# Weight copies moved behind the last attention pair, and both halves of a scatter moved ahead of it

## The reference

```
x = x + tanh(g_xattn) * attention(layernorm(x), ctx)      # 8 batches, 256 tokens, 128 wide, 16 heads of 64
logits = layernorm(x) @ Wr + br ;  i = argmax(logits)     # 8 experts, 512 hidden
out = sum over e of relu((xn * (i == e)) @ W1[e] + b1[e]) @ W2[e] + b2[e]
x = x + tanh(g_ffn) * out
```

## Time and profile before

| | us |
|---|---|
| median of 3 runs | 365.06 (364.78 to 365.91) |
| profiled execution | 365.85 |
| its span, first to last instruction | 363.8 |
| PE busy | 345.6 (95%) |
| DVE busy | 270.9 (74%) |
| ACT busy | 255.5 (70%) |
| POOL busy | 191.0 (52%) |
| mean granted TensorE clock | 0.998 |

### The profile page before, as it was taken

The page is one execution under the profiler, slowest core; times in us unless marked ns, Lnnn a source line. Parts: engine busy times, 40 slices in busy tenths (PEclk is TensorE's granted clock), DMA queues, the critical chain, the costliest instruction groups (busy, mean ns, idle before and its releaser), DMA issues.

```text
span 363.8 us, 11160 instructions
## 1 busy us (share of the span) xinstructions
PE 345.6 (95%) x2835; PEld 283.3 (78%) x2835; DVE 270.9 (74%) x1262; ACT 255.5 (70%) x936; POOL 191.0 (52%) x369
## 2 busy tenths in 40 slices
PE   8999999999999999999999999999999897978893
PEld 6776778778878787878778877887887666968893
DVE  4789995878687868786878687867777696776671
ACT  3686775887687868785878587859773667646562
POOL 7245555366537744774467436833681570345544
PEclk9999999999999999999999999999999999999999
DMA  6999202000400030004000400040005914133320
GB/s 201 248 367 244 91 2 90 4 2 1 122 0 0 0 119 0 0 0 119 0 0 0 119 0 0 17 117 0 0 29 211 366 36 133 50 104 105 89 66 13
DMA packets 21562, 27.87 MB, mean 77 GB/s; under 512 B 3649, under 2 KB 16789, under 8 KB 21536
## 3 DMA queue, kind: packets, MB, share of 16 engines
q1 hardware_dynamic: 19776, 23.85, 21.7%
q0 software_dynamic: 1504, 3.16, 2.5%
q10 hardware_dynamic: 256, 0.56, 0.5%
HBM read 19.00 MB, written 9.01 MB: 77 GB/s over the span
## 4 chain that ended last, share of the span: by engine, by line
PE 80%; DVE 10%; issue 3%; ACT 3%; DVEq 1%; DMA 1%; another core or an unknown queue 1%; POOLq 0%; SPq 0%; POOL 0%; ACTq 0%
PE ps_kv L1255 15%; PE ps_o L1255 13%; PE ps_s L1255 13%; PE ps_t L1359 11%; PE ps_w L1255 10%; PE ps_q L1255 8%; PE ps_t L1255 7%; DVE masked L823 2%; DVE prob_T L842 2%; PE ps_s L1479 1%; ACT prob L565 1%; PE ps_w L1396 1%; DMA nat<-in_ctx 1%; DVE row_fix L830 1%
## 5 line engine op out<-in xcount | busy, mean ns | idle before, releaser
L433 POOL TENSOR_SCALAR prob<-prob,row_inv 128x128 f32<-128x128 f32 (+1 forms) x256 | 104.8, 429 | 124.9 <-DVE row_inv L836 124.7
L565 ACT ACTIVATE prob<-masked,neg_max 128x128 f32<-128x128 f32 (+1 forms) x256 | 113.7, 447 | 65.5 <-DVE neg_max L823 65.2
L823 DVE CUSTOM_DVE_ANT_0 masked<-ps_s,mask_now 128x128 f32<-128x128 f32 (+1 forms) x256 | 77.8, 353 | 44.3 <-PE ps_s L1255 40.8
L842 DVE COPY prob_T<-ps_t 128x384 f32<-128x384 f32 x123 | 65.0, 549 | 0.8 <-PE ps_t L1359 0.7
L1255 PE MATMUL ps_s<-k_T,q_T 64*128 64x128 f32 (+1 forms) x512 | 59.6, 351 | 1.5 <-DVE neg_max L823 1.5
L1359 PEld LDWEIGHTS ps_t<-ident,prob 128*128 128x128 f32 x384 | 41.0, 141 | 21.5 <-issue 17.3
L1359 PE MATMUL ps_t<-ident,prob 128*128 128x128 f32 x384 | 56.1, 282 | 0.6 <-DVE prob_T L842 0.5
L1255 PE MATMUL ps_o<-prob_T,v_nat 128*64 128x256 f32 (+1 forms) x512 | 49.8, 333 | 2.1 <-DVE prob_T L842 1.5
L565 ACT ACTIVATION_READ_ACCUMULATOR prob<-masked,neg_max 128x1 f32 x256 | 48.5, 190 | 0.0
L1255 PEld LDWEIGHTS ps_o<-prob_T,v_nat 128*64 128x64 f32 x512 | 31.7, 136 | 16.3 <-issue 2.1
L1255 PEld LDWEIGHTS ps_s<-k_T,q_T 64*128 64x128 f32 x512 | 33.9, 188 | 9.7 <-issue 6.8
(11 more groups left out here) (200 smaller groups left out, 545.9 us busy)
## 6 DMA issues: line engine op xcount, KB each, us to landing
ctx_buf<-in_ctx SPq DMA_DIRECT2D x8, 768.0 KB
sorted_rows<-pad_rows SPq DMA_DIRECT2D x8, 642.5 KB, 4.4
tile_in<-sorted_rows SPq DMA_DIRECT2D x24, 128.5 KB, 2.1
packs<-in_L_ffn_W SPq DMA_DIRECT2D x1, 2048.0 KB
packs<-in_L_ffn_W SPq DMA_DIRECT2D x8, 256.0 KB
nat<-in_ctx SPq DMA_DIRECT2D x8, 128.0 KB, 3.4
nat<-in_x SPq DMA_DIRECT2D x1, 768.0 KB, 6.6
w_in<-in_L_xattn_Wk SPq DMA_DIRECT2D x2, 256.0 KB, 4.5
```

The source lines that it names most:

```text
L433: g.tensor_scalar(prob[:, slot, lo:hi], prob[:, slot, lo:hi], row_inv[:, slot, t:t + 1], 1.0, ALU.mult, ALU.mult).then_inc(prob_ready, 1)
L565: s.activation(prob[:, slot, lo:hi], masked[:, slot % 2, lo:hi], ACT.Exp, bias=neg_max[:, slot, t:t + 1], scale=-1.0, accum_out=row_sum[:, ...
L823: v.tensor_tensor_reduce(out=masked[:, slot % 2, lo:hi], in0=ps_s[slot % 2][:, lo:hi], in1=mask_now[:, lo:hi], scale=-SCALE, scalar=FLOOR, ...
L842: v.tensor_copy(prob_T[:, slot % TSLOTS, :], ps_t[slot % 2][:, 0:W3]).then_inc(probT_kept, 1)
```

## The change

Three moves; no work is added or taken away.

DVE: the w2 copies of tiles 0 to 3 come behind the copy of pair 63's first head. The other three leave the batch: tile 4's stands behind the second norm of batch 7, tile 5's behind `choose`, tile 6's behind `place`.

ACT: in the batch only the w1 copy of tile 0 stays, at the end of j = 6, behind the copy of pair 63's second head. The other six come after tile 0's transposed copy: two at once, then one in each of the turns of tiles 0 to 3, ahead of that tile's hidden operations.

POOL: the second indirect DMA of batch 6's scatter goes ahead of `normalise` of pair 63, together with the first.

```diff
@@ POOL @@
-            def scatter(b, tiles=range(QT)):
+            def scatter(b):
...
-                        scatter(b - 1, [0])
-                    if last and j == 5:
-                        scatter(b - 1, [1])
+                        scatter(b - 1)
@@ ACT @@
-                    if last and j == 5:
+                    if last and j == 6:
                         act.wait_ge(early_table_ready, 1)
                         act.wait_ge(ld_ffn, 16 * (E + 2))
-                        for tile in range(2):
-                            early_w1(tile)
-                    if last and j == 6:
-                        for tile in range(2, 5):
-                            early_w1(tile)
+                        early_w1(0)
...
             keep_tileT(0, 0)
-            early_w1(5)
+            for tile in range(1, 3):
+                early_w1(tile)
             for tile in range(EARLY):
                 if tile < EARLY - 1:
                     keep_tileT(tile + 1, tile + 1)
-                if tile == 1:
-                    early_w1(6)
+                if tile + 3 < EARLY:
+                    early_w1(tile + 3)
                 act.wait_ge(w1_early, tile + 1)
                 keep_hidden(tile, tile)
@@ DVE @@
             for step in range(12):
                 second_norm(B - 1, step, ps_q)
+            early_w2(4)
             dve.wait_ge(rest_loaded, 16)
...
                 choose(B - 1, step)
+            early_w2(5)
             early_rest(2)
             for step in range(4):
                 place(B - 1, step)
+            early_w2(6)
             finish(2, 2)
...
-EARLY_W2 = (34, 35, 36, 37, 40, 41, 42)
+EARLY_W2 = (38, 39, 40, 41)
```

More of the change, by code:

```diff
@@ L458, in residual_of @@
                                 ).then_inc(residual_ready, 1)
-            def scatter(b, tiles=range(QT)):
+            def scatter(b):
                 pool.wait_ge(slots_ready, b + 1)
                 settle(pool)
-                for t in tiles:
+                for t in range(QT):
                     g.indirect_dma_start(out=sorted_rows[:, :],
```

## The result

| | before | after |
|---|---|---|
| median of 20 runs | 364.97 us (362.96 to 368.56) | 368.19 us (366.21 to 370.32) |
| profiled execution, its span | 365.85, 363.8 | 367.15, 364.6 |
| mean granted clock of that run | 0.998 | 0.993 |

The ratio is 1.0085 (1.0065 to 1.0106): the change costs 3.1 us. Forecast was 365.4, with a range of 364.1 to 366.6 and a chance of 0.21 for slower, so the prediction was wrong.

What follows compares the result with a forecast made beforehand. PE was taken as the bound, nearly full from tile 7, whose load waits for the late table. The 1.4 us early gain is given back, leaving +0.35 there: 365.06 + 0.35 = 365.4 us, range 364.1 to 366.6.

Steps and rivals of the forecast that it cites:

- picture of tile 7: Tile 7's load waits for scatter and late table; the table is the later path, with 0.2 allowed for both being level.
- the table path: DVE's late table, read by SP before tile 7's load: +0.2 at best, +0.65 at worst of the likely cases.
- what the early stage gains: Last pair: value products 1.45 us sooner, second norm 1.4 us sooner; the late table gives it back with a little more.
- tile 6's copy: DVE's w2 copy between the slots and tile 2's finish and late table: nothing hides it, the table path pays 1.05.
- ACT didn't become the bound: Slower rival, tiles 0 to 3: exposed number loads delay hidden(2) to 313.9 or later; 366.1 to 366.5, 0.21 over the 1.1 line.
- Tile 0's load: Ahead of the last projection on PE: there at 303.5, wanted at 304.0; 0 taken, 0.3 us as upper end.
- 0.28 that the scatter's issue might pay: Last batch's scatter on POOL beside tile 6's DVE copy: can take 0.28 longer, with 0.6 or more to spare.
- cost 0: POOL's second scatter issue ahead of pair 63's normalise: no cost; without cover, at most the 0.9 us normalise moves.
- cover for `normalise`: Pair 63's transposes wait for DVE's copy to 300.20 anyway, leaving 0.4 us of cover for the later normalise.
- The sum at tile 7's load: Table path of +0.2 to +0.65, up to 0.2 of it free if the load waited for the scatter; +0.35 taken.
- The end moves by as much as tile 7's load moves: From tile 7 on PE is nearly full, so the load's shift, not the last pair's gain, sets the end.

Runs made afterwards that it cites:

- a_six: The changed kernel with tile 6's w2 copy moved from DVE to ACT, behind tile 4's hidden operations: 364.84 us, ratio 0.9997.
- b_pool: The kernel before with only POOL's part of the change, both halves of batch 6's scatter ahead of pair 63's normalise: 362.88 us, ratio 1.0017.
- a_fill: The changed kernel plus unused PE products, four ahead of tile 6's second product and five ahead of tile 7's transpose: 365.25 us, ratio 1.0028.
- a_six_fill: The changed kernel with tile 6's w2 copy on ACT and unused PE products, four before tile 6's second product, three before tile 7's transpose: 361.82 us, ratio 0.9983.
- b_late_fill: The kernel before with two more SP table reads ahead of tile 7's load and seven unused PE products before its transpose: 366.08 us, ratio 1.0018.
- best_table: a_six_fill with steps 2 to 7 of DVE's early table moved behind the copy of pair 62's first head: 364.55 us, ratio 0.9949 against before.
- a_again: The changed kernel unaltered, timed again beside before on another chip, with a second profile: 368.61 us, ratio 1.0071.
- a_act_back: The changed kernel with only ACT's w1 copies put back, DVE and POOL staying changed: 367.92 us, ratio 1.0064.
- a_pool_back: The changed kernel with only POOL's part undone, the second scatter issue back in its old place: 365.05 us, ratio 1.0082.
- b_late: The kernel before with two more SP table reads between the scatter's landing and tile 7's load: 364.85 us, ratio 1.0066.
- a_dve_back: The changed kernel with only DVE's w2 copies put back, ACT and POOL staying changed: 364.64 us, ratio 1.0009.

## Why the prediction was wrong

**Its picture of tile 7 was right.** In after the table path is the later one, and what the early stage gains is given back by tile 6's copy: from slot_i to the last step of the late table it is 4.81 in after and 3.74 in before, 1.07 more, where 1.05 was forecast; a_six takes it away again. In before the two paths were level, with the scatter the later by 0.13: the load's issue ends 1.48 behind the table's last step there and 1.35 in after. The forecast had allowed up to 0.2 for this. ACT didn't become the bound: PE has the ranks at 313.5 and DVE takes them at 314.21, and hidden(2) is over at 312.35, ahead of the 312.85 to 313.5 that I had worked out. Tile 0's load hid, as forecast. Of the 0.28 that the scatter's issue might pay beside tile 6's copy, 0.09 shows: it takes 1.05 in after and 0.96 in a_six.

**The step that failed first: "cost 0" for POOL's move.** It rested on cover for `normalise` at the transposes. The cover was there, and `normalise` starts where it was said to (+2.41; the forecast's 298.7 is +2.44). But DVE's table steps in front of pair 62's copy became longer, and with it everything to the second norm: 0.59 gained there (10.05 to 9.46) in place of 1.4. By the ranks nothing is left of it (+0.05), the table is 1.11 late, and all but the 0.13 by which the scatter held the load before reaches PE: 0.97. So the move priced at 0 cost 0.87 at pair 62's copy, and that is the failed term. In b_pool, with none of the other moves, the 0.87 loses more than half to DVE's wait for the ranks. In the change tile 5's copy and a rest fill that wait, so nothing takes it up. The sum at tile 7's load was +0.35 and measured +0.97. I had allowed 0.9 as the upper bound of this very edit, but for `normalise`'s own delay and not for DVE's steps beside it.

**The step that was missing: the clock.** "The end moves by as much as tile 7's load moves" takes PE's speed for given. PE idles 0.95 and 1.15 us just ahead of tile 7, where before idled once, 1.32, and had tile 7 all but without a wait. The earlier trace rows has the clue: 0.18 of waiting for the load, so every delay of it becomes a new idle time of PE, behind a second product that isn't late any more. The windows and the profile's clock row stood at full speed up to PE's last product, so I read the clock as no part of the sum; a full clock in one profiled run isn't a clock that holds in every run. Before has a fall in 39 of its 99 runs with a recorded clock, the change in 23 of 32, the four kernels with fillers at both gaps or ahead of tile 7 (a_fill, a_six_fill, b_late_fill, best_table) in 0 of 48. The Trainium skill (TensorE: Matmul & The Clock Gate, "Part 1: The HAM clock gate (the "warmup" mystery)") says that the clock follows how busy PE has been; the traces agree in that the clock goes from 1.00 to 0.50 behind the gaps in after, a_again and a_act_back and stays at 1.00 where they are filled, and don't show a rule, since in a_pool_back it stays at 1.00 behind the same gaps.

**The sum as measured.** In the two profiled executions, from the first scatter issue on: tile 7 comes 0.97 later, PE is busy 1.38 longer behind it, and idles 0.67 less. That is 1.68; less the 0.89 of chance ahead of it the span is 0.8 longer, and with 0.5 more outside the span the run is 1.3 longer. Over many runs the change has before's clocks beside it only in a_again, so what follows is an estimate from 12 runs and 35. Its mean span is 1.64 above before's (365.83 against 364.19). Its mean clock is 0.9903 against 0.9932, worth 0.7 to 1.0 by the straight line of b_late's section; the rest, 0.6 to 0.9, is near the delay at tile 7. Outside the span it has 0.67 more by the means. So the theory that the clock makes 2 us of the 3 isn't borne out: the loss has three parts of 0.6 to 1.0 each, and the clock is one of them. By a_fill, whose interval is 0 to 2 us, no split can be told.

**What stays open.** The part outside the span has no cause here. It is 2.59 in the change and 2.66 in a_again, against 1.78 in before beside it, but 1.80 in a_fill and 1.87 in a_act_back, which still loses 2.3 us; it is 2.62 in a_six, which loses nothing, 2.63 in a_pool_back and 2.67 in b_late, with 2.33 in before beside these two. Before itself has it between 1.7 and 2.9 in single runs. No edit of mine was aimed at it, and no part of the change goes with it.

PE's standstills in the expert tiles are open too: from 9 us behind tile 7 on there are none over 0.3 in the four profiled runs on the second chip, and two of 1.23 and 1.46 in b_late_fill on the third; they move a single profile's span by up to 2.7 us.

Open, last, is what stretches the table's steps. The Trainium skill (SBUF — State Buffer, "Who interferes with whom") says that a DVE instruction with two SBUF inputs contends with a GpSimd instruction that reads SBUF. The rows agree only in part: two of the three stretched steps have two inputs, but `before_e` has one, which this sentence doesn't cover. In a_pool_back, as in before, the second scatter is away from the table and the same steps run beside `normalise` (from 297.27) at full speed, so `normalise` alone doesn't do it; but `early_e` is stretched in b_pool when the second issue has ended. No run here has the second scatter beside the table without `normalise` behind it.

## What to carry to other kernels

Compare two traces from the last event that the edit can't have moved, not from the span's start; here 0.9 us of chance in front of it made a loss look like the gain that was forecast. Where a late transfer ends in an idle PE ahead of a long stretch bound by PE, price the clock too: look at how long PE idles there in all, and expect the fall in a share of the runs, whatever one profile shows. A handful of unused products in such a gap took the falls away in the four kernels that had them ahead of tile 7; it isn't free (an estimated 0.36 us of tile 7 in best_table), and as a test it tells a delay from a clock only if it is compared with runs of the other kernel that hold their clock too.

## What the runs showed of the hardware

- Gaps of 0.95, 1.15, 0.37 and 0.37 us with full work between them came ahead of a fall to 0.50, and so did one of 2.15 (b_late); 1.06 or 1.32 with 0.37 twice did not in the profiled runs of a_dve_back and before. The border is not a sharp one: 1.39, 0.33 and 0.37 came ahead of a fall in a_six, and 0.95, 1.20, 0.37 and 0.37 did not in a_pool_back. PE's busy time from tile 7 on is 33.2 to 33.5 in after, a_again and a_six, 34.3 to 34.6 in b_late and a_act_back, whose falls are longer, and 31.3 to 32.3 in the nine profiled runs without a fall.
- 7 to 9 unused products (14 to 18 instructions) in those gaps, 1.7 to 2.3 us in all, kept the clock at 1.00 in the profile and at 0.995 or over in 47 of 48 runs' means.
- Steps of 8 to 56 elements on DVE, 0.15 to 0.27 long, took 0.42 to 0.53 beside POOL's second indirect DMA and the `normalise` behind it (b_pool, after), and kept their length beside `normalise` alone (a_pool_back).
- DVE's copy with a register load in front starts 0.75 behind the step before it (slot_i at 314.90, copy at 315.65), and the time of a run outside its span takes values from 1.7 to 3.0 us.
